# Layer-norm row statistics stored as table columns, and a node stage whose gathered sum moves to TensorE

## The reference

```
h  = relu(layernorm(x))                      # in front of every layer, per row: (x - mean) / sqrt(var + 1e-5)
x1 = x  + relu([h, mean of edge MLPs] @ W3 + b3) @ W4 + b4       # layer 0
x2 = x1 + layernorm(attention(h1) + h1) * gamma + beta           # layer 1, attention summed over the edges into a node
x3 = x2 + relu(sum over edges and self of dis*dis * (h2 @ W.T + b))   # layer 2, dis = 1/sqrt(degree)
out = x3 + (edge-weighted sums of h3 @ Wg + bg) @ Wfc.T + bfc    # layer 3
```

## Time and profile before

| | |
|---|---|
| median of three runs | 3022.01 us (3018.73 to 3023.68) |
| span of the profiled execution, which is its own time on the page | 3096.9 us |
| PE / PEld busy | 2274.6 us (73%) / 2008.0 us (65%) |
| DVE busy | 1744.5 us (56%) |
| ACT / POOL busy | 1089.9 us (35%) / 970.3 us (31%) |
| DMA | 330.20 MB, mean 107 GB/s |

### The profile page before, as it was taken

The page is one execution under the profiler, slowest core; times in us unless marked ns, Lnnn a source line. Parts: engine busy times, 40 slices in busy tenths (PEclk is TensorE's granted clock), DMA queues, the critical chain, the costliest instruction groups (busy, mean ns, idle before and its releaser), DMA issues. The chain is left out here.

```text
span 3096.9 us, 40519 instructions
## 1 busy us (share of the span) xinstructions
PE 2274.6 (73%) x13127; PEld 2008.0 (65%) x13127; DVE 1744.5 (56%) x3459; ACT 1089.9 (35%) x1842; POOL 970.3 (31%) x762
## 2 busy tenths in 40 slices
PE   6989999999995999999996996510000165899466
PEld 6979898989895888888885875410000154777355
DVE  4633232323234544445443657879999367999444
ACT  2234333333343343333332554323333263333232
POOL 1001010000003322232313341655665504565565
PEclk9989999999997999999997998765555577999778
DMA  6101010101023232322323231234432534665443
GB/s 200 34 8 55 18 51 17 51 17 50 20 49 145 103 114 95 142 114 94 98 90 123 82 96 42 92 144 146 149 133 101 174 127 178 245 245 222 141 139 119
DMA packets 111202, 330.20 MB, mean 107 GB/s; under 512 B 25980, under 2 KB 39292, under 8 KB 90570
## 3 DMA queue, kind: packets, MB, share of 16 engines
q1 hardware_dynamic: 61628, 228.63, 19.6%
q0 software_dynamic: 42976, 99.20, 10.9%
q10 hardware_dynamic: 6530, 1.53, 0.2%
HBM read 247.80 MB, written 128.41 MB: 121 GB/s over the span
## 5 line engine op out<-in xcount | busy, mean ns | idle before, releaser
L1914 PE MATMUL f_c_ps<-f_zeros 128*40 128x258 f32 x4 | 1.9, 641 | 389.2 <-DVE f_heads L1369 389.2
L1914 PEld LDWEIGHTS f_c_ps<-f_zeros 128*40 128x40 f32 x4 | 0.6, 174 | 390.2 <-DVE f_heads L1369 389.7
L135 PE MATMUL b_y_ps<-W23h,b_Rh 128*128 128x320 f32 x800 | 249.7, 312 | 0.0
L136 PE MATMUL b_y_ps<-W23l,b_Rh 128*128 128x320 f32 x800 | 246.4, 308 | 0.6 <-issue 0.6
L137 PE MATMUL b_y_ps<-W23h,b_Rl 128*128 128x320 f32 x800 | 246.6, 308 | 0.2 <-issue 0.2
L536 POOL DMA_INDIRECT b_X<-in_x,b_idx x40 | 40.3, 1008 | 635.0 <-PE b_tp_ps L716 624.4
L135 PE MATMUL b_hid_ps<-b_hTh,W1h 128*128 128x512 f32 x500 | 201.4, 403 | 7.9 <-ACT b_Rh L585 7.9
L135 PE MATMUL c_u_ps<-c_W3h,c_hTh 128*128 128x320 f32 x640 | 201.2, 314 | 0.0
L136 PE MATMUL b_hid_ps<-b_hTl,W1h 128*128 128x512 f32 x500 | 200.2, 400 | 0.0
L137 PE MATMUL b_hid_ps<-b_hTh,W1l 128*128 128x512 f32 x500 | 200.0, 400 | 0.0
L137 PE MATMUL c_u_ps<-c_W3h,c_hTl 128*128 128x320 f32 x640 | 198.0, 309 | 0.0
(11 more groups left out here) (383 smaller groups left out, 7238.5 us busy)
## 6 DMA issues: line engine op xcount, KB each, us to landing
c_X<-in_x SPq DMA_DIRECT2D x21, 1024.0 KB
x<-n_O SPq DMA_DIRECT2D x20, 1032.0 KB, 4.0
g_X<-x SPq DMA_DIRECT2D x20, 1032.0 KB
x<-c_XB SPq DMA_DIRECT2D x20, 1024.0 KB, 4.2
n_X<-x SPq DMA_DIRECT2D x20, 1024.0 KB
x<-g_O SPq DMA_DIRECT2D x20, 1024.0 KB, 3.9
c_XB<-in_x SPq DMA_DIRECT2D x19, 1024.0 KB
out<-g_B SPq DMA_DIRECT2D x19, 1024.0 KB
```

The costliest lines, as they stand in the source:

```text
L135: pe.matmul(out, ah, bh, start=first, stop=False)
L136: pe.matmul(out, ah, bl, start=False, stop=False)
L1914: pe.matmul(c[0:ET, h, 0:HW], zeros[:, 0:ET], zeros[:, :], start=True, stop=False)
```

## The change

1. Stage c computes, for each finished x1 row, `1/sqrt(var + eps)` and `-mean` times that, and stores them as two more columns of x1 (rows of 514 in place of 512).
2. Stages d and n read these columns as scale and bias of the normalisation; their own statistics of x1 go. In d the semaphore of a gather is split into one for the source rows and one for the destination rows, and ACT waits for them.
3. Stage n is written anew, a group of four tiles at a time, with constants in place of loop registers. PE makes `diag(has) @ G + I @ H` in float32 into PSUM (two products per tile, eight buffers), ACT makes the diagonal matrices D, DVE takes the statistics from PSUM, ACT normalises from PSUM into N. Gamma and the residual are one DVE instruction each per group (2048 elements). Three G buffers and four X buffers; the gather of group g + 3 waits for the products of group g. DVE takes statistics of the x2 rows and stores scale and shift, times `dis`, in the table's last two columns, which held `dis`.
4. Stages f and g read those; their statistics, roots and scales go. In f, ACT no longer copies out of PSUM: DVE copies both halves in one instruction of 516 columns. f's loops are written out, and the waits for a T buffer's store are there only from the second use of a buffer on.

Core of the diff:

```diff
 # c, layer0_nodes: DVE, fourth part of a round (stats1 of the rows 0 to 3 stand likewise behind add_residual)
+                def stats1(r, b, j):
+                    t = GROUP * b + j
+                    dve.wait_ge(o_out, r * GT + (t + 1 + 2))
+                    dve.bn_stats(one["raw"][:, t, :], XB[:, b, j, 0:F]).then_inc(out_step, 1)
+                def scale1(r, b):
+                    dve.wait_ge(std1_ready, r * 2 + (b + 1))
+                    dve.reciprocal(XB[:, b, :, F:F + 1], one["std"][:, n].unsqueeze(2)).then_inc(out_step, 1)
...
                     for j in range(GROUP):
                         add_residual(r, 1, j)
+                        if j == 0:
+                            stats1(r, 0, GROUP - 1)
+                            mean1(r, 0)
                         turned_rows(r + 1, (2 * j, 2 * j + 1))
+                        if j == 0:
+                            scale1(r, 0)
+                        else:
+                            stats1(r, 1, j - 1)
+                    stats1(r, 1, GROUP - 1)
+                    mean1(r, 1)
+                    scale1(r, 1)
 # c, SP
-                    sp.wait_ge(o_out, r * GT + (4 * b + 4 + 2))
-                    sp.dma_start(group_rows(x1, g, F), XB[:, b, :, :]).then_inc(stored[b], 16)
+                    sp.wait_ge(x1_ready, r * 2 + (b + 1))
+                    sp.dma_start(group_rows(x1, g, XV), XB[:, b, :, :]).then_inc(stored[b], 16)
 # n, layer1_nodes: POOL
+                def gather(g):
+                    if g >= RG:
+                        pool.wait_ge(z_ready, GROUP * (g - RG) + GROUP)
...
+                for g in range(NG):
+                    pool.wait_ge(h_ready, GROUP * g + GROUP)
+                    pool.tensor_tensor(X[:, g % RX, :, 0:F], X[:, g % RX, :, 0:F], wide(beta), ALU.add).then_inc(res_ready, 1)
+                    if g + RG < NG:
+                        gather(g + RG)
 # n, DVE
+                stats2(0)
+                scale2(0)
+                for g in range(NG):
+                    if g + 1 < NG:
+                        stats2(g + 1)        # 4 bn_stats of z in PSUM, 4 bn_aggr
+                    if g:
+                        scale3(g - 1)        # columns F+2 and F+3 of x2
+                    weigh(g)                 # N *= gamma, 2048 elements
+                    if g + 1 < NG:
+                        scale2(g + 1)
+                    add(g)                   # O = N + X, 2048 elements
+                    stats3(g)                # 4 bn_stats of O, 4 bn_aggr
 # n, PE
+                for g in range(NG):
+                    pe.wait_ge(run_loaded[g % RG], 64 * (g // RG + 1))
+                    pe.wait_ge(d_ready, GROUP * g + GROUP)
+                    if g >= 2:
+                        pe.wait_ge(n_ready, GROUP * (g - 2) + GROUP)
+                    for j in range(GROUP):
+                        i = GROUP * (g % 2) + j
+                        pe.matmul(z[:, i, :], D[:, g % 2, j, :], G[:, g % RG, j, :], start=True, stop=False)
+                        pe.wait_ge(h_ready, GROUP * g + j + 1)
+                        pe.matmul(z[:, i, :], keep["ident"][:, :], H[:, g % 2, j, :], start=False, stop=True).then_inc(z_ready, 1)
 # f, layer2_edges: DVE
-                dve.tensor_copy(T[0:ET, 0, 0:HW], c[0:ET, 0, 0:HW]).then_inc(t_out[0], 1)
+                def out(t):
+                    dve.wait_ge(sum_ready, t + 1)
+                    if t >= GROUP:
+                        dve.wait_ge(stored[j], 16 * (t // GROUP))
+                    dve.tensor_copy(halves(T[:, j, :]), s[:, 2 * (t % RS):2 * (t % RS) + 2, 0:HW]).then_inc(t_out, 1)
+                for t in range(ET):
+                    if t % GROUP == 0 and t + GROUP < ET:
+                        mask(t // GROUP + 1)      # waits for the next four gathers
+                    if t + 2 < ET:
+                        split(t + 2)
+                    out(t)
 # g, layer2_nodes: DVE, all that is left of statistics and scale
+                    dve.tensor_tensor(sc[:, u % 2, :, :], X[:, u, :, F + 2:XW],
+                                      over(keep["dis"][:, bass.ds((it * RING + u) * GROUP, GROUP)].unsqueeze(2), [P, GROUP, 2]),
+                                      ALU.mult).then_inc(norm_ready, 1)
```

More of the change, by code:

```diff
@@ L1226, in _ @@
                         turned(g + 1, 1 - b, 0, (0, 1), g * 4)
-                        root(g + 1, 1)
                         message(g, 3)
                         turned(g + 1, 1 - b, 0, (2, 3), g * 4)
-                        norm_rows(g + 1, 1 - b, 1, range(GROUP))
+                        norm_rows(1 - b, 1, range(GROUP), loaded)
             @block.vector
             def _(dve):
[L1235 to L1251, removed]
                 def turned(g, b, q, chunks):
@@ L1568, in layer1_nodes @@
     sem = core.sem
[L1569 to L1574, removed]
@@ L1583, in layer1_nodes @@
         O = sb("O", [P, 2, GROUP, XW])
-        idx = sb("idx", [P, GT], I32)
-        one, two = core.stats(st, "n1"), core.stats(st, "n2")
+        two, three_ = core.stats(st, "nz"), core.stats(st, "no")
         gamma, beta = sb("gamma", [P, F]), sb("beta", [P, F])
[L1588 to L1594, removed]
@@ L1608, in body @@
[L1608 to L1616, removed]
-                rounds(sp, body)
-                sp.wait_ge(stored, 16 * NG)
+                load(2)
@@ L1676, in _, with present, norm1 @@
-                norm1(0, 0)
-                rounds(act, body)
+                def present(g):
+                    if g >= 2:
+                        act.wait_ge(z_ready, GROUP * (g - 2) + GROUP)
+                    for j in range(GROUP):
+                        t = g * GROUP + j
+                        act.activation(D[:, g % 2, j, :], keep["ident"][:, :], ACT.Identity,
+                                       scale=keep["has"][:, t:t + 1]).then_inc(d_ready, 1)
+                def norm1(g, rows):
+                    act.wait_ge(x_loaded[g % RX], 16 * (g // RX + 1))
+                    for j in rows:
+                        x = X[:, g % RX, j, :]
+                        act.activation(H[:, g % 2, j, :], x[:, 0:F], ACT.Relu, bias=x[:, F + 1:F + 2],
+                                       scale=x[:, F:F + 1]).then_inc(h_ready, 1)
@@ new lines, in root, with norm2 @@
+                def root(g, s, var, std):
+                    act.wait_ge(var, GROUP * g + GROUP)
+                    act.activation(s["std"][:, both(g)], s["mv"][:, both(g), 1], ACT.Sqrt, bias=keep["eps"][:, 0:1]).then_inc(std, 1)
+                def norm2(g):
+                    act.wait_ge(z_norm, g + 1)
+                    if g >= 2:
+                        act.wait_ge(summed, g - 1)
+                    for j in range(GROUP):
+                        i = GROUP * (g % 2) + j
+                        act.activation(N[:, g % 2, j, :], z[:, i, :], ACT.Identity, bias=two["shift"][:, i:i + 1],
+                                       scale=two["rstd"][:, i:i + 1]).then_inc(n_ready, 1)
@@ new lines, in scale2, with weigh @@
+                def scale2(g):
+                    n = both(g)
+                    dve.wait_ge(z_std, g + 1)
+                    dve.reciprocal(two["rstd"][:, n], two["std"][:, n]).then_inc(z_step, 1)
+                    dve.wait_ge(z_step, 5 * g + 5)
+                    dve.scalar_tensor_tensor(out=two["shift"][:, n], in0=two["mv"][:, n, 0], scalar=-1.0, in1=two["rstd"][:, n],
+                                             op0=ALU.mult, op1=ALU.mult).then_inc(z_norm, 1)
+                def weigh(g):
+                    dve.wait_ge(n_ready, GROUP * g + GROUP)
+                    dve.tensor_tensor(N[:, g % 2, :, :], N[:, g % 2, :, :], wide(gamma), ALU.mult).then_inc(times_gamma, 1)
```

510 lines of the change are left out of this document (208 added, 302 removed).

## The result

The changed kernel takes 2903.25 us (median of four runs, 2899.24 to 2907.34) beside 3022.85 for the kernel before on the same chip: a ratio of 0.9609, 95% interval 0.9585 to 0.9633, so -120 us. The forecast was 2868, in a range of 2820 to 2935.

The account below looks back on a forecast made before the run. The prediction took n as bound by DVE, f by a wait, g by DVE and PE in turns, PE bounding d. Terms +6 - 5 - 75 - 50 - 34 = -158 us, scaled to -154, gave 2868 us, range 2820 to 2935.

Parts of the forecast that it names:

- c, +6: Stage c, first node stage: added x1 statistics mostly hidden beside PE; store 4 us later plus small exposures, +6 us.
- the next loads of X, all needed microseconds later: Stage c: work queued behind the new waits, including the next X loads, is needed only microseconds later; part of +6.
- Rival D: Stage c: the new DVE work shows, +70 in place of +6; kernel 2930 us; chance 0.08.
- d, -5: Message stage d: statistics leave DVE but PE is the bound; only one early gather wait can go, -5 us.
- n, -75: Second node stage n, rewritten: 13.5 us per group of four tiles, 308 us against 383, -75 us.
- rival B: Stage n: DVE alone bounds it, 11.5 us per group, n at 268, -115; kernel 2829 us; chance 0.18.
- The half addition of 2 us per group: Stage n: DVE's two-input passes and POOL's beta exclude each other, costing half a beta per group: 13.5 us, not 11.5.
- That gathers get through: Stage n: POOL's gathers are not excluded by DVE's two-input passes; four gathers at 1.30 us pitch, POOL 9.7 with beta.
- f, -50: Edge stage f: statistics, roots and waits before the copies out go; gathers at 1.30 us pitch; -50 us.
- Rival F: Stage f keeps its 10 us waits, -25 in place of -50; kernel 2892 us; chance 0.08.
- g, -34: Third node stage g: PE's idle wait for g_A goes, 1.5 us over 18 groups, plus twice 3.5 at the start; -34 us.
- The scaling by 0.976: Whole kernel: median 3022.0 is 0.976 of the profiled span 3096.9, so the summed -158 us became -154.

Follow-up runs that it names:

- the reordered run: Changed kernel with c's b4 addition cut in four, g's fourth-row g_A moved ahead of finish and bias, and eight load semaphores in f: 2833.11 us.

## Why the prediction was right in total and wrong by its steps

*c, +6: wrong, +50.* The step that ended "the next loads of X, all needed microseconds later" failed. It asked when the loads are needed, and not what their landing triggers: POOL's `b4` additions, 4.4 us of mean each, which follow the residual load and shut out DVE's two-input pass. The late addition then cost 34 us of PE's waits and 14 us more of its busy time at the lower clock. That the store goes 4 us later was right; that DVE's added work has cover was right too (c is 681 us with it once the addition is cut). Rival D had about the size, +70, and another reason; the sign that the prediction named against itself, PE's waits for DVE in c growing by tens of microseconds, came (8.3 to 42.0). By the Trainium skill ("SBUF — State Buffer", section "Who interferes with whom") issue order, not the kind of operation, decides who blocks; the 7.03 us pair behind an addition that began 2.3 us earlier agrees.

*d, -5: mis-sized, -16.* The early wait is 5.4 by itself, as priced; the chain from statistics to normalised rows was taken as free beside PE, and was not (another 5.4 by itself). The other 7 us of its loop are open.

*n, -75: the mechanism of rival B, not the forecast's.* B said 11.5 us per group and -115; the trace shows 11.4 in most groups, and the windows -105. B's number is in part luck: DVE's own work is 10.9 us, and 0.5 is exclusion that B left out. The half addition of 2 us per group was the forecast's mis-sized term: 0.9 of mean by the run without `beta`. That gathers get through was wrong too: half of them are held up, which fills POOL's 9.7 us per group up to 11.4. PE's products ran beside DVE as assumed, 167 us in 20 groups or 8.4 each, at a granted clock of 0.80 over the stage, so for the larger part at 2.4 GHz and not at 1.2.

*f, -50: wrong, -24.* Its base was wrong: 137 us in the recorded trace, with 10 us waits that this kernel doesn't have in its other profile, 112 us. The forecast for the stage itself, 80 to 95 us, was met (87.7), though not by its reasons: the gathers went at 1.7 us and not at 1.30, held by four under way, and the DMA engines were not the limit (76.5 us with more buffers). Rival F's -25 came about without F's mechanism: no 10 us wait was left to keep.

*g, -34: the term of 1.5 us per group was mis-sized.* Over 20 groups the period went from 14.1 us of mean to 13.3 (POOL's additions: 2548.5 to 2815.7 before, 2444.7 to 2697.2 after); the 14.3 of the earlier trace rows is one pair. That is 0.8 us and not 1.5, because the wait for `g_A` was only in part statistics; the rest was DVE's order, which the reordered run gave back (-12, a period of 12.6). The start gave 6 of the 7 us that were priced.

*The scaling by 0.976* spread the excess of the recorded execution over all stages. Most of it, 70 of 80 us, lay in d, f and h.

## What to carry to other kernels

When a store or load is made later, follow the queue behind it to what its landing starts, and look at which engine's instruction that start will now meet; a delay of 4 us that seemed hidden cost 50. Long POOL instructions that read SBUF beside DVE passes with two SBUF inputs are best cut into pieces where another engine waits for DVE, and left whole where DVE itself is the bound. A profile that is some per cent longer than the median is taken again before its idle stretches become terms of a sum.

## What the runs showed of the hardware

DVE's two-input passes do not only wait for POOL's addition: they also hold up POOL's gathers. In n a gather that started inside such a pass ended 0.9 us behind the pass and took 1.88 or 2.22 us where 1.00 is its best, and the earlier trace rows had one of 9.18. In most groups of n no instruction of POOL follows a wait for a semaphore; by this reading such holds, and not a semaphore, put `beta` into DVE's time without long two-input passes, but no run separates that.

In c, PE's stands of up to 3.9 us cost more than their own length: 34 us of waits came with 14 us more of busy time for the same 3872 records, at a granted clock of 0.95 in place of 0.98; with the addition cut it is 648 us again.

57 us of DVE's statistics passes and aggregates (49.3 and 7.4) could be put back into d without moving its loop by more than 0.1 us, while one wait of 9.2 us at the head of DVE's queue made PE stand 3.7 us in one piece, most of the 5.4 that the early waits cost.
